# Query loads of the loop issued from the scalar engine's queue in step two

## The chip, the cores and the metric

The kernel runs on one core of a Trainium2 chip. The metric is the device time of one execution in microseconds: the median of several runs is 1070.59 us for the kernel before. The core has five engines that run their own instruction streams and meet only through semaphores: PE (matmuls, with PEld for its weight loads), DVE (vector), ACT (scalar, activation functions), POOL (GpSimd) and SP (which here only issues DMAs). DMAs move data between HBM and the on-chip memory; SP and ACT each have a queue of their own from which they can issue them.

## What is computed

The reference is one decoder layer on 32 batches of 56 tokens of width 128, with a context of 1500 rows per batch: self-attention, cross-attention with 16 heads of width 8 and a relative position bias, and a gated feed-forward block, each followed by a residual and a layer norm. The part around the change is the cross-attention:

```
q = shape(query_states @ wq, T)          # T = 56
k = shape(key_value_states @ wk, S)      # S = 1500
v = shape(key_value_states @ wv, S)
scores = einsum('bhtd,bhsd->bhts', q, k) + bias
weights = softmax(scores, axis=-1)
attn = einsum('bhts,bhsd->bhtd', weights, v)
return attn @ wo
```

## The kernel before

`self_attention_block` runs first and leaves the queries of all 32 batches in HBM (`qslots`, seen as `m.qparts`), each split into three bf16 parts so that products in bf16 keep the accuracy of f32. `cross_attention_block` then works through the batches in one software pipeline, and `ffn_block` ends the program.

The cross-attention loop has one pass per batch, `iteration(g, u)`, with u from -1 (which only prepares) to 32 (which only finishes batch 31). A pass is cut into ST = 12 steps j, one per block of 128 context rows. Every engine has the same loop with its own part of each step:

- PE, `scores` (L615): 8 matmuls per step, in two halves of 4, from the key stack `kst` and the query stack `qst` of batch u into the three banks of `st_ps`. `max_chunk` (L100): two matmuls per step that compute scores in the other orientation for a batch ahead, whose row maxima are needed before its exponentials; from step 8 on they belong to batch u + 2, before that to batch u + 1. `value_pair` (L645, L654): in every odd step the exponentials times the values of two steps. And one task per step in the bank `misc`: in steps 0 to 2 the values of the next batch (L696), in step 3 the denominators (L702, L703), in steps 4, 5 and 7 the keys of batch u + 3 (L691), in step 9 the transposed maxima (L673). `misc_free` makes PE wait until the engine that read the task before has emptied `misc`.
- ACT: two exponentials per step (L794, from `st_ps` into `e_sb`), in step 1 the copy of the finished output (L799), and the copies out of `misc`: the values (L771 and L773, `v_copy`, ending in the semaphore `s_ve`), the denominators (L817), the keys (L811, L812).
- DVE: the reductions of the max matmuls (L107, L110), the bias of the near positions (L724), reciprocals.
- POOL: splits the keys into three bf16 parts (L841, L844, L847).
- SP: the DMAs. Per pass in this order: one query load for batch u + 2, six key loads for it (`stack_k`, L85, once the stored parts have landed), five more query loads (`stack_q`, L93), the context of batch u + 4 (L868), the store of the keys' first part (L871), the row of maxima into the query stack (L894), the stores of the other two parts (L871).

The stacks `kst` and `qst` are rings of RING = 3 batches. For one batch, six slots of 16 partitions each are filled, each by a load of its own; a query load is 28 KB, a key load 375 KB. PE waits for all six query loads (`s_q`) and then all six key loads (`m.s_kl`) at the first max matmul of a batch, in step 8. Batches 0 and 1 are loaded ahead of the loop; `later` says that a batch is 2 or above, so 30 passes, b = 0 to 29, hold the loads in question. A slot of the ring is free once the scores of the batch before have been computed, which the wait for `s_st` at 2 * b * ST says.

Of the kernel before, what the change touches and what calls it, by code (L numbers as in the profile page):

```python
# [31 lines left out]
NG = B // GB  # L32
# [4 lines left out]
SLOTS = 6  # L37
# [8 lines left out]
ST = -(-S // P)  # L46
# [4 lines left out]
RING = 3  # L51
# [16 lines left out]
def st_rows(j):  # L68
    return min(P, S - j * P)
# [6 lines left out]
def stack_rows(slot, first=0, lanes=LANES):  # L76

    return slice(STEP * first + slot, STEP * (first + lanes - 1) + slot + 1, STEP)
# [10 lines left out]
def stack_q(sp, d, m, n, u, signal, slots=range(SLOTS)):  # L89

    for slot in slots:
        i = QPART[slot]
        sp.dma_start(m.qst[stack_rows(slot), u % RING, :, :].rearrange("l p c -> l (p c)"),  # L93
                     m.qparts[i, bass.ds(n, 1), :, :].rearrange("n l c -> (n l) c")).then_inc(signal, 16)
# [402 lines left out]
def cross_attention_block(nc, d, m):  # L497

    with ExitStack() as ctx:
# [19 lines left out]
        s_kw, s_q = [sem(f"kw{i}") for i in range(3)], [sem(f"q{r}") for r in range(RING)]  # L519
# [3 lines left out]
        s_st, s_kp, s_vp, s_nt, s_pv, s_dn = (sem(n) for n in ("st", "kp", "vp", "nt", "pv", "dn"))  # L523
# [10 lines left out]
        def batch(g, u):  # L534
            return BODY * g + u

        def run(iteration):

            def whole(eng):
                for b in range(FIRST, B + 1):  # L540
                    iteration(0, b)
            return whole

        def filled(g, n, ring, step):

            return BODY // ring * step * g + step * (n // ring + 1)

        def later(g, n):

            return SA_K <= n < B  # L550

        def wait(eng, s, v):
            if not isinstance(v, int) or v > 0:
                eng.wait_ge(s, v)

        def live(g, n):

            return not isinstance(g, int) or 0 <= n < B
# [24 lines left out]
        def misc_user(g, u, j):  # L583

            user = (HEAD_MISC if u == FIRST else MISC).get(j)
            return user if user and (later if user[0] == "k" else live)(g, u + user[2]) else None
# [174 lines left out]
        @block.scalar  # L761
        def _(act):
            def v_copy(n, u, c):

                act.wait_ge(s_vp, 3 * n + c + 1)
                src = misc[:, :].rearrange("p (i n) -> p i n", i=4)
                dst = m.vals[:, u % 2, 4 * c:4 * c + 4, :]

                parts = ((P, 0, 4),) if c < 2 else ((P, 0, 3), (st_rows(ST - 1), 3, 4))
                for K, a, z in parts:  # L770
                    nc.scalar.copy(dst[0:K, a:z, 0:128].rearrange("p i (g n) -> p i g n", g=4)[:, :, :, 0:24],  # L771
                                   src[0:K, a:z, 0:96].rearrange("p i (g n) -> p i g n", g=4))
                    ins = nc.scalar.copy(  # L773
                        dst[0:K, a:z, 128:192].rearrange("p i (g n) -> p i g n", g=2)[:, :, :, 0:16],
                        src[0:K, a:z, 96:128].rearrange("p i (g n) -> p i g n", g=2))
                ins.then_inc(s_ve, 1)

            def iteration(g, u):
                b = batch(g, u)
                for j in range(ST):  # L780
                    if j == NMT and live(g, u + 1):
                        act.wait_ge(s_nt, b + 2)
                        if live(g, u):
                            act.wait_ge(s_md[u % 2], filled(g, u, 2, 16))
                        nc.scalar.copy(nmp[:, :], misc[0:3 * PAIRS, 0:TT]).then_inc(s_nr, 1)
                    if live(g, u):
                        K = st_rows(j)
                        wait(act, s_pv, b * PAIRED + j // 2 - 1)
                        for h in range(2):
                            w = 2 * (b * ST + j) + h  # L790
                            if j < 2:
                                act.wait_ge(s_nb, 4 * b + 2 * j + h + 1)
                            act.wait_ge(s_st, w + 1)
                            nc.scalar.activation(e_sb[0:K, j % E_RING, h * HALF:(h + 1) * HALF],  # L794
                                                 st_ps[0:K, w % ST_BANKS, 0:HALF], ACT.Exp).then_inc(s_ex, 1)
                    if j == 1 and live(g, u - 1):
                        act.wait_ge(s_pv, b * PAIRED)
                        wait(act, s_xo, b - 1)
                        nc.scalar.copy(x_sb[:, :], pv_ps[:, 0:PIECES * T]).then_inc(s_xr, 1)  # L799
                    user = misc_user(g, u, j)  # L800
                    if user:
                        kind, part, lag = user
                        n = batch(g, u + lag)
                        if kind == "k":
                            act.wait_ge(s_kp, 3 * (n - SA_K) + part + 1)
                            if n > SA_K:
                                act.wait_ge(s_k3, 3 * (n - SA_K - 1) + part + 1)
                            if part == 0:
                                wait(act, s_kw[0], 16 * (n - SA_K))
                            cols = slice(part * CH, (part + 1) * CH)  # L810
                            nc.scalar.copy(kpart[:, 0, cols], misc[:, 0:CH])  # L811
                            nc.scalar.copy(k_left[:, cols], misc[:, 0:CH]).then_inc(s_kf, 1)  # L812
                        if kind == "v":
                            v_copy(n, u + lag, part)
                        if kind == "den":
                            act.wait_ge(s_dn, n + 1)
                            nc.scalar.copy(den[:, :], misc[:, 0:PIECES * T]).then_inc(s_dr, 1)  # L817

            run(iteration)(act)

        @block.gpsimd
# [43 lines left out]
        @block.sync  # L865
        def _(sp):
            def load_ctx(n, u):
                sp.dma_start(ctxt[:, u % RING, :], d["ctxT"][bass.ds(n * C, C), :]).then_inc(s_ctx[u % RING], 16)  # L868

            def store_k(u, i):  # L870
                sp.dma_start(m.kparts[u % RING, i, :, :], kpart[:, i, :]).then_inc(s_kw[i], 16)  # L871

            def iteration(g, u):

                b = batch(g, u)
                if later(g, u + 2):
                    wait(sp, s_st, 2 * b * ST)
                    if u + 2 == SA_K:
                        sp.wait_ge(s_kz, 2)
                    stack_q(sp, d, m, b + 2, u + 2, s_q[(u + 2) % RING], (0,))  # L880
                    for i in range(3):
                        sp.wait_ge(s_kw[i], 16 * (u + 3 - SA_K))
                    stack_k(sp, d, m, u + 2, m.s_kl[(u + 2) % RING])
                    stack_q(sp, d, m, b + 2, u + 2, s_q[(u + 2) % RING], range(1, SLOTS))
                if live(g, u + 4):
                    if live(g, u + 1):
                        sp.wait_ge(s_vp, 3 * (b + 2))
                    load_ctx(b + 4, u + 4)
                if later(g, u + 3):
                    sp.wait_ge(s_kf, 3 * (u + 4 - SA_K))  # L890
                    store_k(u + 3, 0)
                if live(g, u + 1):
                    sp.wait_ge(s_nr, b + 2)
                    sp.dma_start(m.qst[M_ROW:AUG, (u + 1) % RING, :, :],  # L894
                                 nmp[:, :]).then_inc(s_md[(u + 1) % 2], 16)
                if later(g, u + 3):
                    sp.wait_ge(s_kr, 6 * (u + 4 - SA_K) - 1)
                    store_k(u + 3, 1)
                    sp.wait_ge(s_k3, 3 * (u + 4 - SA_K))
                    store_k(u + 3, 2)  # L900

            sp.dma_start(wk[:, :], d["wk"]).then_inc(s_w, 16)
            load_ctx(2, 2)
            load_ctx(0, 0)
            sp.dma_start(wv[:, :], d["wv"]).then_inc(s_w, 16)
            for i in range(2):
                sp.dma_start(sel[:, i, :], d["sel"][i]).then_inc(s_w, 16)
            load_ctx(1, 1)
            for g in range(NG):
                sp.wait_ge(m.s_qd[g], 16 * 6)  # L910
            sp.dma_start(m.wo[:, :, :], d["wo"]).then_inc(m.s_wo, 16)
            sp.dma_start(own[:, :], d["own"]).then_inc(s_own, 16)
            run(iteration)(sp)
            sp.wait_ge(s_xh, 2 * B)

# [341 lines left out]
```

## Time and profile before

| | |
|---|---|
| median of 3 runs | 1070.59 us |
| lowest and highest run | 1064.58 and 1072.39 us |
| the profiled execution | 1073.1 us, span 1071.3 us |
| mean granted clock of PE | 0.948 of full |
| busy share of PE, DVE, ACT, POOL | 88%, 69%, 57%, 36% |
| stretch of the cross-attention's scores | 142.2 to 905.2 us |
| length of a pass there | about 24 us |

The profile is that of one execution. In a timeline a row is one instruction or a run of like ones on one engine; the bracket at its end is the idle time of that engine before it and what ended it. SPq and ACTq are the issues of DMAs, in which the engine's instruction stream is held by the issue and not by the transfer. The landing of a transfer is read from its semaphore. The granted clock is the share of the full 2.4 GHz that PE had in a stretch.

### The profile page before, as it was taken

What the parts mean: (1) busy time and instruction counts of PE and PEld (TensorE: products, weight loads), DVE (VectorE), ACT (ScalarE), POOL (GpSimd) and SP (SyncE); (2) the same over time, 40 slices, a digit from 0 to 9 for tenths busy, and PEclk for the clock granted to TensorE, in tenths of its full rate; (3) what the DMA queues carried; (4) which work ended last, traced back from release to release, by engine and by line L of the source; (5) the groups of instructions that cost most, each with busy time, mean ns of one, the idle gap of its engine ahead of it and who ended that gap; (6) DMA issues with size and microseconds to landing.
All of it is one profiled execution on the core that took longest, in us unless ns stands there. A gap on an engine that the chain in (4) does not pass through costs nothing. (4 is left out here: it accounts for less than half of the span.)

```text
span 1071.3 us, 26028 instructions
## 1 busy us (share of the span) xinstructions
PE 947.7 (88%) x10410; PEld 656.3 (61%) x10410; DVE 735.4 (69%) x1702; ACT 613.2 (57%) x1423; POOL 387.1 (36%) x323
## 2 busy tenths in 40 slices
PE   6864579999989999899999999999999987799996
PEld 3652256666666666666666666667766665555564
DVE  5655558887878888778888888888878873530014
ACT  2311157766767776666777776776767756352232
POOL 5530524554444455545444445555444400000000
PEclk9856689999999999999999999999999989899998
DMA  7608665566566665555566766655666500300001
GB/s 221 207 13 165 118 194 180 167 180 182 167 194 179 200 187 191 181 167 170 190 183 180 209 182 197 184 167 180 182 197 192 162 12 2 111 1 0 1 9 26
DMA packets 56720, 156.13 MB, mean 146 GB/s; under 512 B 23264, under 2 KB 35480, under 8 KB 53528
## 3 DMA queue, kind: packets, MB, share of 16 engines
q1 hardware_dynamic: 56072, 152.84, 49.0%
q8 instruction: 82, 1.34, 0.6%
q10 hardware_dynamic: 528, 1.63, 0.5%
q14 instruction: 38, 0.31, 0.1%
HBM read 111.63 MB, written 42.63 MB: 144 GB/s over the span
## 5 line engine op out<-in xcount | busy, mean ns | idle before, releaser
L794 ACT ACTIVATE e_sb<-st_ps 128x448 f32<-128x448 f32 (+1 forms) x768 | 372.9, 555 | 88.5 <-DVE st_ps L724 59.6
L110 DVE TENSOR_REDUCE cmax<-max_ps 112x1 f32<-112x512 f32 x512 | 334.2, 681 | 110.3 <-PE max_ps L100 110.1
L100 PE MATMUL max_ps<-kst,qst 111*112 111x512 bf16 x760 | 269.1, 396 | 34.1 <-DMA qst<-qslots 19.9
L615 PEld LDWEIGHTS st_ps<-qst,kst 114*128 114x128 bf16 (+1 forms) x3072 | 198.6, 102 | 123.0 <-ACT e_sb L794 54.1
L615 PE MATMUL st_ps<-qst,kst 114*128 114x112 bf16 (+1 forms) x3072 | 233.7, 215 | 33.7 <-ACT e_sb L794 27.6
L107 DVE CUSTOM_DVE_ANT_0 near_out<-max_ps,near_nat 112x476 bf16<-112x476 f32 x248 | 150.6, 650 | 36.2 <-PE max_ps L100 36.0
L854 POOL TENSOR_TENSOR rec<-rec,own 128x280 f32<-128x280 f32 x32 | 21.0, 655 | 406.1 <-DVE rec L750 406.1
L645 PE MATMUL pv_ps<-e_sb,vals 128*32 128x168 f32 (+1 forms) x3072 | 151.7, 315 | 0.0
L100 PEld LDWEIGHTS max_ps<-kst,qst 111*112 111x112 bf16 x760 | 85.1, 132 | 77.0 <-issue 36.3
L841 POOL TENSOR_TENSOR kpart<-k_left,kpart 128x500 bf16<-128x500 f32 x90 | 122.3, 1358 | 23.9 <-ACT k_left L812 21.7
L811 ACT CAST kpart<-misc 128x500 bf16<-128x500 f32 x90 | 51.8, 575 | 111.1 <-PE misc L691 111.1
L696 PEld LDWEIGHTS misc<-wv,ctxt 128*128 128x128 f32 (+1 forms) x768 | 98.2, 190 | 18.1 <-ACT vals L773 11.4
L696 PE MATMUL misc<-wv,ctxt 128*128 128x128 f32 (+1 forms) x768 | 105.4, 280 | 1.2 <-issue 0.8
L645 PEld LDWEIGHTS pv_ps<-e_sb,vals 128*32 128x32 f32 (+1 forms) x3072 | 81.4, 110 | 40.2 <-ACT e_sb L794 20.1
L847 POOL TENSOR_TENSOR kpart<-k_left,kpart 128x500 bf16<-128x500 f32 x90 | 102.3, 1136 | 7.1
L844 POOL TENSOR_TENSOR k_left<-k_left,kpart 128x500 f32<-128x500 f32 x90 | 102.3, 1136 | 7.0
L691 PE MATMUL misc<-ctxt,wk 128*128 128x500 f32 x180 | 92.2, 593 | 4.6 <-DMA sel<-in_sel 4.2
L654 PE MATMUL pv_ps<-e_sb,vals 128*32 128x112 f32 (+1 forms) x1536 | 73.1, 262 | 0.0
L1130 DVE TENSOR_TENSOR y<-ff_ps,s 112x512 f32<-112x512 f32 x4 | 2.8, 691 | 97.2 <-PE ff_ps L1028 97.2
L771 ACT COPY vals<-misc 128x384 f32<-128x384 f32 (+2 forms) x128 | 51.1, 400 | 21.9 <-PE misc L696 21.9
L724 DVE TENSOR_TENSOR st_ps<-st_ps,near_t 18x144 f32<-18x144 f32 (+1 forms) x128 | 53.4, 460 | 12.7 <-PE st_ps L615 12.6
L654 PEld LDWEIGHTS pv_ps<-e_sb,vals 128*32 128x32 f32 (+1 forms) x1536 | 50.8, 111 | 5.0
(128 smaller groups left out, 930.0 us busy)
## 6 DMA issues: line engine op xcount, KB each, us to landing
kst<-kparts SPq DMA_DIRECT2D x192, 375.0 KB, 6.3
kparts<-kpart SPq DMA_DIRECT2D x90, 375.0 KB, 2.7
ctxt<-in_ctxT SPq DMA_DIRECT2D x32, 750.0 KB, 7.4
qst<-qslots SPq DMA_DIRECT2D x192, 28.0 KB, 6.4
qslots<-qst SPq DMA_DIRECT2D x4, 672.0 KB, 10.2
kparts<-kst SPq DMA_DIRECT2D x6, 375.0 KB, 3.4
h<-in_h SPq DMA_DIRECT2D x2, 1024.0 KB, 8.8
vals<-in_ctxT ACTq DMA_DIRECT2D x2, 750.0 KB, 9.4
```

The source lines that it names most:

```text
L100: return nc.tensor.matmul(dst[0:TT, 0:hi - lo], m.qst[0:M_ROW, r, p, :], m.kst[0:M_ROW, r, p, lo:hi], start=True, stop=True)
L107: return nc.vector.tensor_tensor_reduce(out=m.near_out[:, p % MAX_BANKS, :], in0=src[0:TT, 0:FIRST_CH], in1=m.near_nat[:, p, :], scale=1.0 ...
L110: return nc.vector.tensor_reduce(m.cmax[:, r, c, p:p + 1], src[0:TT, 0:BOUND[c + 1] - BOUND[c]], AX.X, ALU.max)
L615: mm = nc.tensor.matmul(st_ps[0:K, w % ST_BANKS, p * TT:(p + 1) * TT], m.kst[0:AUG, u % RING, 4 * h + p, j * P:j * P + K], m.qst[0:AUG, u ...
L645: nc.tensor.matmul(pv_ps[32 * q:32 * q + 32, 0:A_COLS], m.vals[0:K, u % 2, j, 32 * q:32 * q + 32], e_sb[0:K, j % E_RING, q * A_COLS:(q + 1 ...
L654: mm = nc.tensor.matmul(pv_ps[32 * q:32 * q + 32, A_COLS:A_COLS + B_COLS], m.vals[0:K, u % 2, j, 32 * (4 + i):32 * (5 + i)], e_sb[0:K, j % ...
L691: nc.tensor.matmul(misc[:, 0:CH], wk[:, :], ctxt[:, r, part * CH:(part + 1) * CH], start=True, stop=True).then_inc(s_kp, 1)
L696: mm = nc.tensor.matmul(misc[0:st_rows(t), i * C:(i + 1) * C], ctxt[:, r, t * P:t * P + st_rows(t)], wv[:, :], start=True, stop=True)
L794: nc.scalar.activation(e_sb[0:K, j % E_RING, h * HALF:(h + 1) * HALF], st_ps[0:K, w % ST_BANKS, 0:HALF], ACT.Exp).then_inc(s_ex, 1)
L841: nc.gpsimd.tensor_tensor(kpart[:, 1, cols], k_left[:, cols], kpart[:, 0, cols], ALU.subtract).then_inc(s_kr, 1)
L844: nc.gpsimd.tensor_tensor(k_left[:, cols], k_left[:, cols], kpart[:, 0, cols], ALU.subtract).then_inc(s_kr, 1)
L847: nc.gpsimd.tensor_tensor(kpart[:, 2, cols], k_left[:, cols], kpart[:, 1, cols], ALU.subtract).then_inc(s_k3, 1)
```

## The change

The six query loads of a later batch leave SP's part of the loop. ACT issues them instead, in step 2, between its two exponentials of that step and its copies out of `misc`. The wait for the free ring slot goes with them; the one for `s_kz` and the waits for the stored keys stay with SP. ACT also waits, once ahead of its loop, for the queries' stores to HBM, which SP had waited for and still does.

```diff
@@ -793,6 +793,9 @@
                                                  st_ps[0:K, w % ST_BANKS, 0:HALF], ACT.Exp).then_inc(s_ex, 1)
+                    if j == 2 and later(g, u + 2):
+                        wait(act, s_st, 2 * b * ST)
+                        stack_q(act, d, m, b + 2, u + 2, s_q[(u + 2) % RING])
                     if j == 1 and live(g, u - 1):
@@ -816,6 +819,8 @@
+            for g in range(NG):
+                act.wait_ge(m.s_qd[g], 16 * 6)
             run(iteration)(act)
@@ -877,11 +882,9 @@
                     if u + 2 == SA_K:
                         sp.wait_ge(s_kz, 2)
-                    stack_q(sp, d, m, b + 2, u + 2, s_q[(u + 2) % RING], (0,))
                     for i in range(3):
                         sp.wait_ge(s_kw[i], 16 * (u + 3 - SA_K))
                     stack_k(sp, d, m, u + 2, m.s_kl[(u + 2) % RING])
-                    stack_q(sp, d, m, b + 2, u + 2, s_q[(u + 2) % RING], range(1, SLOTS))
```

On SP, one pass of the loop before: `kparts<-kpart` are key stores, `kst<-kparts` key loads, `qst<-qslots` query loads, `ctxt<-in_ctxT` the context load.

```order
L894 DMA qst<-nmp 3x8x112
L871 DMA kparts<-kpart 128x1500 x2
L93 DMA qst<-qslots 16x896
L85 DMA kst<-kparts 16x12000 x6
L93 DMA qst<-qslots 16x896 x5
L868 DMA ctxt<-in_ctxT 128x1500
L871 DMA kparts<-kpart 128x1500
```

The same place on SP in the changed kernel:

```order
L897 DMA qst<-nmp 3x8x112
L876 DMA kparts<-kpart 128x1500 x2
L85 DMA kst<-kparts 16x12000 x6
L873 DMA ctxt<-in_ctxT 128x1500
L876 DMA kparts<-kpart 128x1500
```

The two groups of query loads are gone, and the context load stands right behind the key loads.

On ACT, steps 1 to 3 of a pass before (`e_sb<-st_ps` are exponentials, `vals<-misc` the value copies, `den<-misc` the denominators):

```order
L799 COPY x_sb<-pv_ps 128x280
L771 COPY vals<-misc 128x4x4x24
L773 COPY vals<-misc 128x4x2x16
L794 ACTIVATE e_sb<-st_ps 128x448 x2
L771 COPY vals<-misc 128x3x4x24
L773 COPY vals<-misc 128x3x2x16
L771 COPY vals<-misc 92x4x24
L773 COPY vals<-misc 92x2x16
L794 ACTIVATE e_sb<-st_ps 128x448 x2
L817 COPY den<-misc 128x280
```

The same place on ACT in the changed kernel:

```order
L802 COPY x_sb<-pv_ps 128x280
L771 COPY vals<-misc 128x4x4x24
L773 COPY vals<-misc 128x4x2x16
L794 ACTIVATE e_sb<-st_ps 128x448 x2
L93 DMA qst<-qslots 16x896 x6
L771 COPY vals<-misc 128x3x4x24
L773 COPY vals<-misc 128x3x2x16
L771 COPY vals<-misc 92x4x24
L773 COPY vals<-misc 92x2x16
L794 ACTIVATE e_sb<-st_ps 128x448 x2
L820 COPY den<-misc 128x280
```

Six issues now stand between the exponentials of step 2 and the four copies that empty `misc` of the third part of the values. PE's and DVE's orders are unchanged.

## Rows read from the trace of the kernel before

**Rows 1.** The page: the span, and PE's busy time.

```profile
span 1071.3 us, 26028 instructions
...
PE 947.7 (88%) x10410; PEld 656.3 (61%) x10410; DVE 735.4 (69%) x1702; ACT 613.2 (57%) x1423; POOL 387.1 (36%) x323
```

**Rows 2.** Waits: who waited for whom, us in total, times, longest.

```profile
PE max_ps L100 <- DMA qst<-qslots: 19.9, 16, 3.2
```

**Rows 3.** DMA issues: how many, KB each, median us from issue to landing.

```profile
kst<-kparts SPq DMA_DIRECT2D x192, 375.0 KB, 6.3
...
qst<-qslots SPq DMA_DIRECT2D x192, 28.0 KB, 6.4
```

**Rows 4.** Timeline of SP: start us, us, tiles, count; last row from another pass.

```profile
526.52 0.33 SPq L871 DMA_DIRECT2D kparts<-kpart  x1
...
534.31 0.53 SPq L93 DMA_DIRECT2D qst<-qslots  x1
536.68 3.65 SPq L85 DMA_DIRECT2D kst<-kparts  x6
540.37 3.11 SPq L93 DMA_DIRECT2D qst<-qslots  x5
543.53 0.58 SPq L868 DMA_DIRECT2D ctxt<-in_ctxT  x1
...
755.48 4.13 SPq L93 DMA_DIRECT2D qst<-qslots  x5
```

**Rows 5.** Timeline of ACT in the same pass, steps 2 and 3.

```profile
536.78 1.00 ACT L794 ACTIVATE e_sb<-st_ps 128x448 f32<-128x448 f32 x2
538.14 0.40 ACT L771 COPY vals<-misc 128x288 f32<-128x288 f32 x1 [0.36 <-PE misc L696]
...
538.70 0.20 ACT L773 COPY vals<-misc 92x32 f32<-92x32 f32 x1
...
540.50 0.39 ACT L817 COPY den<-misc 128x280 f32<-128x280 f32 x1 [0.72 <-PE misc L703]
```

**Rows 6.** Timeline of PE and its weight loads, step 3 of the same pass.

```profile
538.65 0.78 PE L645 MATMUL pv_ps<-e_sb,vals 128*32 128x168 f32 x16
539.55 0.42 PE L100 MATMUL max_ps<-kst,qst 111*112 111x512 bf16 x1
539.60 0.41 PEld L702 LDWEIGHTS misc<-x_sb,sel 128*128 128x128 f32 x2
```

**Rows 7.** Timeline of the kernel's start: first issues of both queues.

```profile
0.73 0.41 ACTq L380 DMA_DIRECT2D rel<-in_rel_bias  x1
...
0.73 0.41 SPq L182 DMA_DIRECT2D wqkv<-in_w_attn  x1
1.17 0.44 ACTq L380 DMA_DIRECT2D onehot<-in_onehot  x1
```

**Rows 8.** Timeline of PE: five of the 16 waits for query loads.

```profile
258.45 0.61 PE L100 MATMUL max_ps<-kst,qst 111*112 111x476 bf16 x2 [1.82 <-DMA qst<-qslots]
309.13 0.61 PE L100 MATMUL max_ps<-kst,qst 111*112 111x476 bf16 x2 [2.30 <-DMA qst<-qslots]
453.67 0.61 PE L100 MATMUL max_ps<-kst,qst 111*112 111x476 bf16 x2 [2.28 <-DMA qst<-qslots]
550.65 0.61 PE L100 MATMUL max_ps<-kst,qst 111*112 111x476 bf16 x2 [1.14 <-DMA qst<-qslots]
861.29 1.04 PE L100 MATMUL max_ps<-kst,qst 111*112 111x476 bf16 x2 [3.24 <-DMA qst<-qslots]
```

**Rows 9.** Windows after four of them: busy (count) per engine, clock, DMA, GB/s.

```profile
260.00:264.00 4.00, 4.00 (x44) 2.71 (x40) 2.42 (x9) 2.31 (x6) 3.78 (x4) 0.60 0.23 87
309.00:311.00 2.00, 1.87 (x36) 1.45 (x36) 1.43 (x5) 0.48 (x2) 1.88 (x2) 1.00 0.21 81
453.50:458.00 4.50, 4.33 (x46) 2.96 (x47) 2.28 (x7) 1.12 (x4) 4.26 (x5) 0.62 0.15 58
861.20:867.00 5.80, 5.71 (x47) 3.77 (x48) 2.64 (x9) 1.89 (x5) 0.00 (x0) 0.50 0.00 1
```

## The prediction

> **What bounds the kernel now.** I read the page's span and busy times first, then the waits of the loop, then the timelines of one pass of the loop on SP, ACT and PE. PE is busy for 947.7 us of a span of 1071.3 us [rows 1], so whatever stops PE in the loop comes almost whole out of the end time, and work elsewhere counts only when PE waits for it. The wait that the change aims at is in the waits view: PE's max matmuls (L100) waited 19.9 us, 16 times, at most 3.2 us, for the query load [rows 2]. All are at the first max matmul of a new batch, in step 8. The timeline of SP shows why the query is late: one query load goes out at 534.31, then SP sends six key loads in 3.65 us from 536.68, and only then the other five query loads in 3.11 us from 540.37 [rows 4]. A query load lands 6.4 us after issue in the median, a key load 6.3 us [rows 3]; for the batch loaded there PE had waited 1.14 us when it went on at 550.65 [rows 8].
>
> **What the change removes.** In each of the 30 passes that load a later batch (b = 0 to 29), SP no longer issues six query loads. Key loads keep their time: they were held by the landing of the split keys (SP is silent from 534.84 to 536.68 [rows 4]), not by the query load ahead of them. The context load that followed at 543.53 moves up to about 540.4, right behind the key loads; nobody was waiting for it, so I cost that at nothing. If it cut into the key loads' landing it would show at step 8. The query loads now leave ACT from about 537.3 and are out before 541; with the landing time of today, 6.4 us [rows 3], they are there by 547.5, about 2 us before PE asks (550.65 less the wait of 1.14 is 549.5 [rows 8]). What is late next is the last key load: issued by 540.3, landing at 546.6, 2.9 us before 549.5. So I take all 19.9 us as gone. With them goes some lost clock: PE ran below full clock after three of the four waits of 1.8 us or more. The granted clock was 0.60 for 4 us after the wait of 1.82 us, 0.62 for 4.5 us after the 2.28 us, 0.50 for 5.8 us after the 3.24 us, and it stayed at 1.00 after the 2.30 us [rows 8, 9]. 1.00 is the level of 2.4 GHz, 0.50 that of 1.2 GHz. The work lost in these is 0.40 x 4 + 0.38 x 4.5 + 0.50 x 5.8 = 1.6 + 1.7 + 2.9 = 6.2 us. Removed in all: 26 us.
>
> **What it adds.** ACT takes six issues between the exponentials of step 2 and the copies of the third part of the values (L771, L773). Its explicit wait is for scores of the previous batch and is long met. An issue holds the sequencer, so all that stands behind it in the program is held: the value copies of step 2, the exponentials of step 3, the denominator copy. The first of them that PE needs are the value copies: PE's denominator matmul (L702) goes into the same bank, misc, and waits until they are out.
>
> The sum, on the pass of 534 to 543 us. The two exponentials of step 2 run from 536.78 to 537.78 [rows 5]; the second starts near 537.3, and I let the issues begin there, since the sequencer is free once it has handed that instruction on. Five query loads took SP 3.11 us, 0.62 each [rows 4]; six take 3.7 us, to 541.0. The value copies take from 538.14 to 538.90 today, 0.76 us [rows 5], so they end at 541.8. PE comes to the denominator at 539.60 (its weight load [rows 6]) and finds the copies done 0.7 us earlier. Now it waits until 541.8: 2.2 us. Before that point it loses nothing: the scores of step 3, two max matmuls and the first value pair need exponentials of steps 0 to 2 only. Afterwards PE and ACT go on at the same distance from each other as today (ACT has an idle of 0.72 us ahead of the denominator copy [rows 5] that is used up), so nothing of the 2.2 us is won back: PE has little idle time to win it from. 30 passes x 2.2 = 66 us.
>
> The new stop is as long as the waits after which the clock fell in three cases of four. It stands alone in a pass and behind fully packed work, where I have no row; I assume a fall in one pass of three, at the 1.65 us that the two shorter falls cost: 10 x 1.65 = 17 us. The ends are no fall (0) and one in each pass (50).
>
> Net: 66 + 17 - 26 = 57 us slower. The profiled execution took 1073.1 us with its span of 1071.3; 57 more is 1130. The median of the runs is 1070.59, 2.5 lower, and by it the forecast is 1128.
>
> **Bounds of the price of an issue.** No row shows a query load issued by ACT. Below: the shortest issue of the loop, a key store of SP, took 0.33 us [rows 4]; six end at 539.3, the copies at 540.0, the stop is 0.45 us and costs 14 us, which leaves a gain of 12. ACT's own issues at the start of the kernel took 0.41 us and came 0.44 us apart [rows 7], of another shape (whole rows of a weight, 32 partitions): six end at 539.9, the stop is 1.1 us, 33 us in all, which leaves 7 us of loss, 1078. Above: the slowest five query loads took SP 4.13 us, 0.83 each [rows 4]; if besides the issues start only when the exponentials are over at 537.78, they end at 542.8 and the stop is 3.9 us, 118 us in all, with falls of the clock up to 168, less 26: 1213. I take 0.62 as it is the row of the same transfer.
>
> **ACT beside SP.** The six issues fall into the same 3.65 us in which SP sends its six key loads. Rows 7 have both queues issuing at once, ACT's first taking 0.41 us and SP's first also 0.41 us, both starting at 0.73: no sign that one holds the other up. The Trainium skill says otherwise (Perfetto Trace Analysis, section "DMA Instruction — HWDGE (DVE, Sync)"): the block that makes the descriptors is locked for one sequencer's use at a time, and the profiled span of an issue contains the wait for that lock. The rows at the start don't bear this out as far as two small loads can tell; by that rule the loss would be that of the second rival below.
>
> **Rivals.**
> Issues are cheap or overlap with ACT's work (not slower). The copies of the values may slip 0.7 us before PE notices, and 30 passes can lose 0.87 us each before the 26 us are used up. So the point is a last issue over by 539.7: 2.4 us for six, 0.40 each, if they begin at 537.3; or 0.62 each if they begin at 536.0, ahead of the exponentials. For it: the row of 0.33 us. Against it: the queries' own rows. With no stop left the time is 1070.6 - 26 = 1045.
> The two queues take turns (much slower). Six issues of ACT and six of SP in one line need 3.65 + 3.7 = 7.4 us, to 544.7, copies over at 545.4; a stop of 5.8 us, 30 x 5.8 + 30 x 1.65 - 26 = +198: 1268. For it: both run in the same 3.7 us. Against it: rows 7.
> The keys are late in place of the queries. Then the wait at step 8 stays and only its name changes: the 26 us are not gained, 1154. For it: both land 6.3 to 6.4 us after issue on the same engines. Against it: keys have 2.9 us to spare, and the stop in step 3 gives them 2.2 us more.
> The change does nothing measurable, because the stop is about 0.9 us: inside 1060 to 1081, between the first rival and the row of ACT's own issues.
>
> **How the numbers follow.** My forecast, a stop of 1.6 to 3.0 us per pass and 1100 to 1185 us: 0.62. A short stop, 1060 to 1100: 0.17, of which 0.10 below 1081. Cheap issues, below 1060: 0.08. Keys late: 0.05. Queues in turn, or anything above 1185: 0.08. A measurement of this kernel can tell about 1%. Faster by over 1%: 0.08. Within 1%: 0.10. Slower: 0.82. The range of 1078 to 1185 leaves out about a tenth on either side; its low end is the price of ACT's own issues, its high end a stop of 3.0 us with a fall of the clock in each pass, less the gain (90 + 50 - 26 = 114).
>
> **What would show it.** Right: query loads under ACT's queue, six in a row, 0.5 to 0.7 us each, with ACT's L771 copy some 3 us later after the exponentials; PE idle of about 2.2 us ahead of L702, 30 times, released by ACT's copies; no wait for query loads at step 8; some stretches of lower clock in the middle of the loop. Wrong: issues of ACT near 0.3 us; ACT copies that start within 0.7 us of today's distance; issues of SP's key loads stretched well past 3.65 us for six (the queues share something); a wait of PE for key loads at step 8.

## The result and the profile after

The changed kernel takes 1115.51 us in the median (1113.95 to 1117.43, 4 runs) against 1067.88 us for the kernel before, measured beside it (1064.58 to 1072.39, 4 runs). The ratio is 1.0444, 95% interval 1.0394 to 1.0494: slower, by 47.6 us between the medians. The profiled executions stand at 1114.95 and 1073.1 us, 41.9 apart, with spans of 1112.9 and 1071.3 us, 41.6 apart. The forecast was 1128 us, with a range of 1078 to 1185.

The page's span and busy times after, to be read beside [rows 1]:

```profile
span 1112.9 us, 26060 instructions
...
PE 952.6 (86%) x10410; PEld 651.2 (59%) x10410; DVE 734.5 (66%) x1702; ACT 612.4 (55%) x1423; POOL 387.5 (35%) x323
```

PE is busy for 4.9 us more and idle for 36.7 us more. The waits view of the changed kernel (engine, tile and line, releaser: us in total, times, longest) says where:

```profile
ACT vals L771 <- issue: 88.3, 30, 3.8
PEld st_ps L615 <- ACT e_sb L794: 66.2, 147, 1.9
PEld misc L702 <- ACT vals L773: 54.2, 29, 2.7
PE misc L702 <- ACT vals L773: 45.6, 29, 2.4
...
PE st_ps L615 <- ACT e_sb L794: 38.4, 67, 1.7
```

The row of [rows 2], L100 waiting for a query load, is gone. In its place stands L702, the denominator matmul, waiting for ACT's value copies 29 times, and ACT itself sat idle 88.3 us ahead of those copies, "issue" being the name for time in which it waited for nothing that the profile shows: its instruction stream was busy with DMAs. The third difference is easily missed. PE's wait for exponentials at L615 was 27.6 us before, in the same view:

```profile
PE st_ps L615 <- ACT e_sb L794: 27.6, 52, 1.0
```

It is 38.4 us now. The sum of PE's idle times is 45.6 more at L702, 19.9 less at L100, 10.8 more at L615: 36.5 us, and with the 4.9 us of busy time 41.4 of the span's 41.6 us.

The span hides a little of the loss. From the first scores (L615) to the last, the loop took 762.9 us before (142.2 to 905.1) and 809.7 now (138.1 to 947.8), 46.8 more; the stretch ahead of it, which does the same work in both, was 4.1 us shorter in this trace and the one behind it 1.1. Of the 46.8 us in the loop 37.7 are idle time of PE and 9.1 busy time. Some 3 us of that are the two matmuls of L702, which take 0.55 us together behind a stop and 0.45 without one, and 4.6 us the keys' matmuls (L691, 610 against 582 ns each), which come some 1.4 us behind L702, where the clock is low in six passes (from 513.53 the two take 1.73 us instead of 1.00).

One pass of the changed kernel on ACT (start us, us, tiles, idle before), to be read beside [rows 5]:

```profile
534.36 0.27 ACT L773 COPY vals<-misc 128x128 f32<-128x128 f32 x1
534.38 0.49 ACTq L93 DMA_DIRECT2D qst<-qslots  x1
534.51 0.56 ACT L794 ACTIVATE e_sb<-st_ps 128x448 f32<-128x448 f32 x1
534.91 0.61 ACTq L93 DMA_DIRECT2D qst<-qslots  x1
534.95 0.56 ACT L794 ACTIVATE e_sb<-st_ps 128x448 f32<-128x448 f32 x1
535.54 2.73 ACTq L93 DMA_DIRECT2D qst<-qslots  x4
538.31 0.40 ACT L771 COPY vals<-misc 128x288 f32<-128x288 f32 x1 [2.80 <-issue]
```

The issues stand behind the two exponentials in the program and yet begin at 534.38, before the first of these starts: the instruction stream runs ahead of the arithmetic. They last 3.9 us, and the copies begin right behind. PE in that pass, beside [rows 6]:

```profile
537.27 0.42 PE L100 MATMUL max_ps<-kst,qst 111*112 111x512 bf16 x1
539.12 0.55 PE L702 MATMUL misc<-x_sb,sel 128*128 128x168 f32 x2 [1.42 <-ACT vals L773]
...
545.85 0.37 PE L615 MATMUL st_ps<-qst,kst 114*128 114x112 bf16 x4 [0.57 <-ACT e_sb L794]
550.13 0.37 PE L615 MATMUL st_ps<-qst,kst 114*128 114x112 bf16 x4 [0.60 <-ACT e_sb L794]
```

Between L100 and L702 PE stands still for 1.42 us (the weight load, which comes first, for 1.72). The two waits of 0.6 us behind it are those for exponentials ahead of the scores of steps 7 and 9. Before, the second was missing behind 14 of the 16 waits for queries, and 0.2 us long behind the two shortest, as ACT had caught up meanwhile.

### The profile page after: what moved, and what is told of

Same layout as the page of the kernel before. It is cut to its first block and busy times, and to the rows that moved or that the text cites. A ratio compares the mean times of both kernels' runs of the same rounds, so it can differ in the third digit from the quotient of the medians.

```text
span 1112.9 us, 26060 instructions
## 1 busy us (share of the span) xinstructions
PE 952.6 (86%) x10410; PEld 651.2 (59%) x10410; DVE 734.5 (66%) x1702; ACT 612.4 (55%) x1423; POOL 387.5 (35%) x323
## 5 line engine op out<-in xcount | busy, mean ns | idle before, releaser
L100 PE MATMUL max_ps<-kst,qst 111*112 111x512 bf16 x760 | 269.1, 396 | 15.6 <-PEq L119 14.6
L615 PEld LDWEIGHTS st_ps<-qst,kst 114*128 114x128 bf16 (+1 forms) x3072 | 198.5, 101 | 137.8 <-ACT e_sb L794 66.2
L615 PE MATMUL st_ps<-qst,kst 114*128 114x112 bf16 (+1 forms) x3072 | 236.0, 215 | 44.3 <-ACT e_sb L794 38.4
L814 ACT CAST kpart<-misc 128x500 bf16<-128x500 f32 x90 | 51.9, 576 | 121.9 <-PE misc L691 121.8
L100 PEld LDWEIGHTS max_ps<-kst,qst 111*112 111x112 bf16 x760 | 85.5, 132 | 56.5 <-issue 36.7
L771 ACT COPY vals<-misc 128x384 f32<-128x384 f32 (+2 forms) x128 | 51.1, 399 | 99.0 <-issue 88.3
L645 PEld LDWEIGHTS pv_ps<-e_sb,vals 128*32 128x32 f32 (+1 forms) x3072 | 80.9, 109 | 40.7 <-ACT e_sb L794 20.3
L691 PE MATMUL misc<-ctxt,wk 128*128 128x500 f32 x180 | 97.0, 621 | 4.6 <-DMA sel<-in_sel 4.2
L702 PE MATMUL misc<-x_sb,sel 128*128 128x168 f32 x64 | 17.9, 362 | 46.2 <-ACT vals L773 45.6
```

The source lines that it names most:

```text
L100: return nc.tensor.matmul(dst[0:TT, 0:hi - lo], m.qst[0:M_ROW, r, p, :], m.kst[0:M_ROW, r, p, lo:hi], start=True, stop=True)
L615: mm = nc.tensor.matmul(st_ps[0:K, w % ST_BANKS, p * TT:(p + 1) * TT], m.kst[0:AUG, u % RING, 4 * h + p, j * P:j * P + K], m.qst[0:AUG, u ...
L645: nc.tensor.matmul(pv_ps[32 * q:32 * q + 32, 0:A_COLS], m.vals[0:K, u % 2, j, 32 * q:32 * q + 32], e_sb[0:K, j % E_RING, q * A_COLS:(q + 1 ...
L691: nc.tensor.matmul(misc[:, 0:CH], wk[:, :], ctxt[:, r, part * CH:(part + 1) * CH], start=True, stop=True).then_inc(s_kp, 1)
```

## Experiments

All ratios are to the kernel before, run beside each. Unless said otherwise the times are medians. Half the dose, behind the copies, in step 5, one per step and ACT but early are edits of the changed kernel; adding alone, GpSimd's queue, queries first and no query loads are edits of the kernel before. A wait or a landing is read from one profiled execution of each. Two of these lie high: that of one per step, at 1068.64 us, and that of queries first, at 1079.03, are each the slowest of their ten, and the profiled execution of the kernel before, 1073.1 us, is 8 us above the medians of the later runs beside it (1064 to 1066). Small differences between traces are therefore weaker evidence than the ratios.

**Adding alone.** The loads stay with SP, and ACT issues six more into a tile of their own (the tile, its semaphore and the waits ahead of and behind ACT's loop are left out here).

```diff
+                    if j == 2 and later(g, u + 2):
+                        wait(act, s_st, 2 * b * ST)
+                        wait(act, s_spare, 16 * SLOTS * b)
+                        for slot in range(SLOTS):
+                            act.dma_start(spare[stack_rows(slot), :],
+                                          m.qparts[QPART[slot], bass.ds(b + 2, 1), :, :].rearrange(
+                                              "n l c -> (n l) c")).then_inc(s_spare, 16)
```

> The kernel before, with SP's query loads as they were, plus six loads of the same shape and size that ACT issues in step 2 into a tile nobody reads. Theory A (the loss is ACT's sequencer being held, and the wait for the queries was worth little because PE would have waited for ACT's exponentials a moment later anyway): the stop ahead of L702 is there, 45 to 55 us in all, the wait of L100 for queries nearly gone although SP still issues them late, since PE comes 1.5 us later; time as the changed kernel, 1108 to 1120 us. Rival B (the two parts of the change add up, and taking the loads from SP gained its 20 us): this one keeps that wait and takes 1130 to 1140 us. Rival C (ACT's issues themselves are harmless, something else in the change costs): 1068 us.

Measured: 1125.39 us, ratio 1.0549 (1.0499 to 1.0598). That is the whole loss of the change and more, with nothing taken from SP. The waits view:

```profile
PE misc L703 <- ACT vals L774: 47.8, 29, 2.9
PE st_ps L616 <- ACT e_sb L795: 35.1, 63, 1.6
...
PE max_ps L100 <- DMA qst<-qslots: 4.9, 4, 2.8
```

The stop is that of the changed kernel (47.8 against 45.6 us), and the wait for SP's queries falls from 19.9 to 4.9 us although they leave as late as ever, because PE comes later. So the two parts of the change don't simply add up, as theory A had it. The time lies between the ranges of theory A and rival B, 5 us from each, so it is the waits that decide. Against the changed kernel the span is 11.9 us longer: 6.5 in the loop (816.2 against 809.7 us), the rest ahead of it and behind it. PE's busy time is 8.3 us above, 3.7 of it in the loop, where more clock was lost (15.4 against 12.0 us, counted as under "Behind the copies").

**Half the dose.** Three loads on ACT in step 2, three on SP behind the keys.

```diff
-                        stack_q(act, d, m, b + 2, u + 2, s_q[(u + 2) % RING])
+                        stack_q(act, d, m, b + 2, u + 2, s_q[(u + 2) % RING], (0, 1, 2))
...
+                    stack_q(sp, d, m, b + 2, u + 2, s_q[(u + 2) % RING], (3, 4, 5))
```

> The changed kernel with only three of the query loads on ACT in step 2, the other three on SP behind the keys. Theory A: the hold is 1.9 us instead of 3.7, the copies slip by about 0.4 us, less than the 0.7 us they had to spare: stop ahead of L702 under 5 us in all, part of the wait for queries left (5 to 12 us), 1058 to 1069 us. A loss in proportion (rival D): half, about 1091 us.

Measured: 1064.13 us, ratio 0.9996 (0.9967 to 1.0024). The wait at L702 is 1.0 us in all (weight loads, twice). A loss in proportion would have been 2.2%; there is none. The cost has a threshold between three and six issues, as expected if the copies may slip by some time before PE notices. The wait for queries stayed larger than expected, 18.3 us.

**Behind the copies.** The six issues moved past the value copies of step 2.

```diff
-                    if j == 2 and later(g, u + 2):
-                        wait(act, s_st, 2 * b * ST)
-                        stack_q(act, d, m, b + 2, u + 2, s_q[(u + 2) % RING])
                     if j == 1 and live(g, u - 1):
...
                             nc.scalar.copy(den[:, :], misc[:, 0:PIECES * T]).then_inc(s_dr, 1)
+                    if j == 2 and later(g, u + 2):
+                        wait(act, s_st, 2 * b * ST)
+                        stack_q(act, d, m, b + 2, u + 2, s_q[(u + 2) % RING])
```

> The changed kernel with the six issues moved behind the value copies of step 2. Theory A (ACT is held for 3.7 us, and the first of ACT's outputs that PE needs decides): no stop ahead of L702, but PE now waits for the exponentials of step 3 (L615, L645) some 1.3 to 2.5 us in each pass, 35 to 65 us more than the 27 us of before, 1095 to 1125 us. If only the copies were the trouble: at most 1070 us.

Measured: 1168.89 us, ratio 1.0954 (1.0902 to 1.1007), worse than forecast. From the timeline of PE and the windows behind the stop (the last columns are granted clock, DMA share, GB/s):

```profile
537.55 0.56 PE L615 MATMUL st_ps<-qst,kst 114*128 114x112 bf16 x4 [3.26 <-ACT e_sb L794]
```

```profile
537.50:541.50 4.00, 3.95 (x17) 2.27 (x17) 2.40 (x3) 2.44 (x6) 0.00 (x0) 0.50 0.83 213
541.50:546.00 4.50, 4.23 (x42) 2.40 (x41) 2.79 (x5) 2.36 (x6) 0.57 (x1) 0.77 0.38 127
```

With the copies in time PE runs on, into the exponentials of step 3, and waits 3.26 us there. So the copies had only been the first of ACT's results to be missed. The pass shown is a bad one: its six issues take 5.07 us against 4.1 on average. Behind its stop the granted clock is 0.50, 1.2 GHz, and it loses 0.50 x 4 + 0.23 x 4.5 = 3 us more. Summed over windows of 4 us from the first to the last scores of each kernel, the clock lost is 46.2 us here, 11.0 before and 12.0 in the changed kernel. The forecast had 35 to 65 us more of waits and nothing for the clock. The whole difference of the spans to the kernel before, 92.8 us, is 77.8 us more of waits for exponentials (105.4 in all), 34.9 us more of busy time at the lower clock, and 19.9 us less of waits for queries.

**In step 5,** when SP's queue is silent; one look.

```diff
-                    if j == 2 and later(g, u + 2):
+                    if j == 5 and later(g, u + 2):
```

> The changed kernel with its six issues in step 5, when SP is not issuing. On the sharing of what makes the descriptors: if the two queues hold each other up, each issue of ACT takes 0.49 to 0.52 us here against the median of 0.61 (longest 1.76) in step 2, six 3.0 us; if not, 0.61 again. The time: the hold is met by PE at the exponentials of step 6 or 7 and the queries come late for step 8: 1095 to 1150 us.

Measured: 1156.27 us, one execution, a little over the range. PE waits 95.9 us for exponentials, at most 3.5 at once, and the loop's lost clock is 51.9 us. The view of the issues' line, from 168 to 850 us:

```profile
L93 ACTq DMA_DIRECT2D qst<-qslots x150: 492/611/1654, 180.0 to 835.4; - x150
```

The median of an issue is 0.611 us with SP silent; it was 0.612 in the changed kernel, beside SP's six key loads. On average it is even longer here, 0.70 us against 0.66. That the queues hold each other up is not what makes an issue 0.61 us long.

**One per step.** One issue behind the exponentials of each of the steps 0 to 5.

```diff
-                    if j == 2 and later(g, u + 2):
+                    if j < SLOTS and later(g, u + 2):
...
-                        stack_q(act, d, m, b + 2, u + 2, s_q[(u + 2) % RING])
+                        stack_q(act, d, m, b + 2, u + 2, s_q[(u + 2) % RING], (j,))
```

> The changed kernel with ACT's six issues spread, one behind the exponentials of each of the steps 0 to 5. Theory A: a hold of 0.6 us fits into ACT's idle time of a step, no stop ahead of L702, the wait for queries gone, the wait for exponentials 35 to 45 us: 1056 to 1066 us, slightly faster than before. Rival D (each issue costs PE its length wherever it stands): about 1150 us. Rival E (the cost is the traffic of a second queue beside the keys): as the changed kernel, 1115 us.

Measured: 1060.85 us, ratio 0.9954 (0.9930 to 0.9979). The same 180 issues on the same queue and no loss. The stop at L702 is gone. The issues' line, again from 168 to 850 us, and the waits:

```profile
L93 ACTq DMA_DIRECT2D qst<-qslots x172: 492/492/530, 168.1 to 847.7; - x172
```

```profile
PE max_ps L100 <- DMA qst<-qslots: 17.3, 15, 2.9
```

A lone issue takes 0.49 us; it is in a row that they take 0.61 and more. Two things missed the expectation: the wait at step 8 did not go, and the one for exponentials stayed at 27.8 us instead of growing.

**ACT, but early.** Three issues ahead of the exponentials of step 0, where ACT idles, one behind those of steps 0, 1 and 2.

```diff
+                    if j == 0 and later(g, u + 2):
+                        wait(act, s_st, 2 * b * ST)
+                        stack_q(act, d, m, b + 2, u + 2, s_q[(u + 2) % RING], (0, 1, 2))
                     if live(g, u):
...
-                    if j == 2 and later(g, u + 2):
+                    if j < 3 and later(g, u + 2):
...
+                        stack_q(act, d, m, b + 2, u + 2, s_q[(u + 2) % RING], (j + 3,))
```

> The changed kernel with three of ACT's issues ahead of the exponentials of step 0, where ACT is idle for 1.9 us in each pass, and one each behind those of steps 0, 1 and 2. Theory A: the place decides, not the queue: ACT is held inside its idle time, no stop ahead of L702 (under 5 us in all), and as the last load leaves in step 2 all land before step 8, so that the wait there is the keys' 6 to 8 us: 1053 to 1062 us. If issuing on ACT's queue beside the keys costs by itself: 1070 us or more.

Measured: 1056.97 us, ratio 0.9937 (0.9906 to 0.9967), as expected. Loads now land after 2.2 us in the median, not 6.2, and PE's wait at step 8 is 8.1 us:

```profile
545.15 1.02 ACT L797 ACTIVATE e_sb<-st_ps 128x448 f32<-128x448 f32 x2 [1.92 <-DVE st_ps L724]
```

The exponentials of step 0 still begin 1.92 us after ACT's last work, as they did: they wait for DVE, and three issues fit in front of them unseen.

**GpSimd's queue.** All six issued by GpSimd at the start of its part of a pass, none by SP (SP's lines go as in the change).

```diff
+                if later(g, u + 2):
+                    wait(pool, s_st, 2 * b * ST)
+                    stack_q(pool, d, m, b + 2, u + 2, s_q[(u + 2) % RING])
                 if live(g, u - 1):
                     pool.wait_ge(s_rc, 2 * b)
```

> The kernel before with the six query loads issued by GpSimd at the start of its part of a pass, where it is idle for 12 us. Neither SP nor ACT is held. Theory A: no stop ahead of L702; the wait at step 8 stays if it is the keys'; 1056 to 1070 us. If the loss of the changed kernel came from taking the loads off SP or from a second queue beside the keys, and not from ACT being held: 1090 us or more.

Measured: 1056.38 us, ratio 0.9897 (0.9849 to 0.9944), faster by 1%. Taking the loads off SP is good by itself. The row below is GpSimd, idle there, paying for it with 2.9 us per pass; then the waits of PE that are left:

```profile
543.64 2.93 POOL L93 DMA_DIRECT2D qst<-qslots  x6
```

```profile
PE st_ps L615 <- ACT e_sb L794: 31.9, 60, 1.0
...
PE max_ps L100 <- issue: 5.9, 8, 1.3
```

**All on SP, queries first.**

```diff
-                    stack_q(sp, d, m, b + 2, u + 2, s_q[(u + 2) % RING], (0,))
+                    stack_q(sp, d, m, b + 2, u + 2, s_q[(u + 2) % RING])
...
-                    stack_q(sp, d, m, b + 2, u + 2, s_q[(u + 2) % RING], range(1, SLOTS))
```

> The kernel before, with all six query loads issued by SP ahead of the key loads, ACT untouched. Theory A: the wait for queries goes, the keys are issued 1 to 2 us later and may be waited for in some passes, and in the others PE's wait for ACT's exponentials in step 8 grows from 27 to about 37 us; gain 0 to 10 us, 1058 to 1068 us. Rival B (the wait was worth all its 20 to 26 us): 1042 to 1048 us if the keys are in time.

Measured: 1069.85 us, ratio 1.0054 (1.0014 to 1.0095): slower by half a percent, 2 us above theory A's range and far from rival B's. The queries land after 2.2 us, and PE waits in step 8 all the same, longer than before. Waits, and SP's timeline:

```profile
PE max_ps L100 <- issue: 30.2, 20, 3.3
```

```profile
533.81 4.53 SPq L93 DMA_DIRECT2D qst<-qslots  x6
538.45 3.68 SPq L85 DMA_DIRECT2D kst<-kparts  x6
```

Here the keys leave 4.6 us after SP began the queries, at 538.45. Before, in [rows 4], they left 2.4 us after the first query load (534.31, then 536.68), so they are some 2.3 us later than they were. So they had little or nothing to spare. The row's "issue" names no releaser; that it is the keys is read from this: nothing else that L100 waits for had moved back. The run without queries, next, has the keys by name.

**No query loads at all** in the loop, nor PE's wait for them.

```diff
-                    if later(g, u + lag):
-                        pe.wait_ge(s_q[r], filled(g, u + lag - SA_K, RING, Q_LOAD))
-                    else:
+                    if not later(g, u + lag):
...
-                    stack_q(sp, d, m, b + 2, u + 2, s_q[(u + 2) % RING], (0,))
...
-                    stack_q(sp, d, m, b + 2, u + 2, s_q[(u + 2) % RING], range(1, SLOTS))
```

> The kernel before without any query load in the loop (PE's wait for them goes too; the scores of batches 2 to 31 are computed from stale queries, so the work on PE, DVE and ACT is the same and the result is not). Theory A2, formed from the one-per-step run, whose wait at step 8 stayed at 17.3 us with the query loads issued long before: the wait is one for the last of the six key loads, which lands much later than the median of the six. Then a wait of 12 to 20 us stays at L100 in step 8, and the time is 1060 to 1068 us. Rival B (it is the queries'): the wait goes, PE waits about 10 us more for exponentials, 1053 to 1058 us.

Measured: 1056.25 us, ratio 0.9915 (0.9883 to 0.9946). The time is in rival B's range; the wait that is left lies between the two forecasts:

```profile
PE max_ps L100 <- DMA kst<-kparts: 6.5, 8, 2.2
```

Without queries PE waits 6.5 us for keys in 8 passes, and its wait for exponentials is 32.4 us. Of the 19.9 us of the row, 6.5 were the keys' anyway and 4.8 come back at L615, which leaves 8.6; by the medians the gain is 9 us. The lost clock went as well: 3.6 us in this loop against 11.0 before, and 1.9 and 1.8 with GpSimd's queue and ACT early. These three loops are 14.5 to 16.6 us shorter than the one before, more than the medians give (7 to 9), since the trace before is of a long execution. So 9 us is about what the removal could bring, clock included; GpSimd's queue brings as much.

**Keys by part.** A key load leaves as soon as its own part is stored (`stack_k` takes the parts to load as an argument), on top of one per step, and on top of GpSimd's queue.

```diff
                     for i in range(3):
                         sp.wait_ge(s_kw[i], 16 * (u + 3 - SA_K))
-                    stack_k(sp, d, m, u + 2, m.s_kl[(u + 2) % RING])
+                        stack_k(sp, d, m, u + 2, m.s_kl[(u + 2) % RING], (i,))
```

> The one-per-step kernel with each key load issued as soon as its own part has landed in HBM, not after all three have: five of the six key loads leave some 2 us earlier. Theory A2 (keys are what step 8 waits for): the wait of L100 falls from 17 us to under 6 us, some of it comes back as waits for exponentials; 1048 to 1058 us, faster than one per step. Rival (the wait is for queries, or DMA throughput alone sets it): the wait stays at 14 us or more and the time within 0.3% of one per step.

Measured: 1055.94 us, ratio 0.9897 (0.9845 to 0.9949); the wait at L100 fell from 17.3 to 7.8 us, not under 6. It had been put down to query loads, and only keys were moved. Yet ACT early, which moved only queries, brought it down as far, to 8.1 us. So neither load alone was what PE waited for: in one per step both landed late, and the row names the one that landed last. How much each holds the other up is not shown, and part of the fall from 17.3 may be the long execution that this number comes from.

> The GpSimd version with the key loads issued as each part has landed. Theory A2 (what is left at step 8 are the last key loads): the 6 us left there go, part of them returns as waits for exponentials: 1050 to 1056 us, 0 to 0.5% faster than the GpSimd version. If the keys' landing is set by throughput: the wait stays at 5 us or more.

Measured: 1058.11 us, ratio 0.9952 (0.9924 to 0.9981): no gain over GpSimd's queue alone, and the wait stayed at 5.5 us. The keys' median landing rose from 6.4 to 8.4 us as they left earlier, which speaks for the expectation's second case, that the transfers themselves are what is left there. Of the versions tried, GpSimd's queue and keys by part with one issue per step have the best ratios, each 1% faster than before, but their intervals overlap with those of ACT early and of no query loads: which of them is best is not shown.

## Why the prediction was right

The direction, the mechanism and the place held: ACT held by six issues, the value copies late, PE stopped ahead of L702. Adding alone shows the loss without the removal, half the dose shows the threshold, one per step shows that the queue itself is harmless. The sum of 57 us against 41.9 (profiled), 46.8 (the loop) and 47.6 (medians) is nearer than its terms deserve: three were off, and they partly cancel.

- **The stop, 2.2 us a pass, 66 us.** Measured: 54.2 us by the weight load in 29 waits, 1.87 each (45.6 by the matmul). I let the issues begin in the middle of the exponentials, at 537.3. They begin 0.13 us before the first one's start, which on the pass of rows 5 is 536.65, 0.65 earlier. They cost a little more than taken, 0.66 us each on average over the timeline against 0.62, or 0.2 us in six. 2.2 - 0.65 + 0.2 = 1.8.
- **The clock, 17 us.** It fell after the stops of 2.38 us at 174.8, 2.01 us at 304.8, 1.91 us at 433.8 and those of 2.14, 2.27 and 1.92 us, not after the many of 1.25 to 1.5 us, nor after those of 1.75, 1.87 and 2.43 us (the last at 228.25). The windows behind three stops, the last one of 1.42 us:

```profile
304.80:308.80 4.00, 4.00 (x20) 2.51 (x21) 2.14 (x3) 2.14 (x6) 0.00 (x0) 0.58 1.03 264
433.80:437.80 4.00, 4.00 (x25) 2.66 (x25) 2.40 (x3) 2.69 (x7) 0.00 (x0) 0.67 0.97 247
539.10:543.10 4.00, 3.98 (x50) 2.86 (x51) 2.57 (x4) 3.61 (x9) 0.00 (x0) 1.00 1.08 298
```

  Six falls came in, 10 us together, not ten with 17; each was about as dear as taken. The three behind waits for queries went with their 6 us, as forecast, and so did a fourth, at 888 us behind a wait of 1.58 us for DVE, that no term had. The loop's lost clock is 12.0 us against 11.0 before, so that terms with a sum of 11 us came to about 1. What I had not thought of is where they fall: the new ones lie on matmuls behind L702, and PE's busy time rose by the 9.1 us above.
- **The removal, 19.9 us of waits: wrong.** Two steps failed. "So I take all 19.9 us as gone" overlooked the wait for exponentials that stood behind the other; it grew by 10.8 us. And "2.9 us before 549.5" for the keys was the median landing of six loads put on the last of them: with the queries first and the keys some 2 us later PE waited 30.2 us, and without queries 6.5 us of key wait stay. The longest landing of a key load before was 10.6 us. By the waits the removal brought 9.1 us here (19.9 less 10.8), and 9 by the medians where no loads are left. In the changed kernel the keys' wait does not show only because PE's stop comes first.

The rival of cheap issues falls: a lone one takes 0.49 us, one in a row 0.61 or more. The rival of queues in turn falls too: 1.8 us of stop and not 5.8, and an issue equally long with SP silent. The Trainium skill (Perfetto Trace Analysis, "DMA Instruction — HWDGE (DVE, Sync)") has the block that makes descriptors locked for one sequencer at a time. Such a lock may exist; the section speaks of DVE and Sync, and these runs leave little for it between ACT and SP: SP's six key loads took 3.91 us on average over 25 passes beside ACT's, 3.78 over 27 before, and ACT's issues were no shorter with SP silent. The rival of late keys was half right, as told above, but in a form that cost gain and not time.

## What to carry to other kernels

A DMA issue was free here on an engine that nothing waited for, or where the issuing engine had time to spare before its next result was needed. Count six issues in a row as an instruction of 4 us, and look for the first result behind them that the bound engine needs, then for the second. Split one per step, or put in front of an instruction that waits anyway, the same issues cost nothing. A wait that is to be removed is worth no more than the time to the next wait on the same engine; take the transfers out altogether once to see that limit, here 9 us where the row said 19.9, and judge a group of loads by the landing of the last, not by the median.

## What the runs showed that I had not expected

ACT's issues don't wait for its arithmetic before them: in the pass shown they begin 0.13 us before the first of the two exponentials that precede them in the program, and overlap with both. The first issue of a row takes 0.49 us, the next 0.61 and some up to 1.76, whether SP issues or not; what makes the long ones was not found, and they are why some stops reach 2.4 us. A query load of 28 KB on ACT's own queue took 6.2 us in the median to land beside the keys and 5.4 in one per step, though its queue held no other loads then, and 2.2 us when it left ahead of the keys: a queue of its own did not get a small load past large ones here.
